# Another order of work inside the attention steps of a fused attention and expert kernel

## The reference

```
Q = LN(x) Wq' + bq;  K = ctx Wk' + bk;  V = ctx Wv' + bv
scores = softmax(Q K' / 4) over 361 keys, per head
x1 = x + tanh(g_x) * (concat_heads(scores V) Wh' + bh)
t  = RMSnorm(LN(x1)) * norm_w;  two best of 8 experts per token
x2 = x1 + tanh(g_f) * sum over 2 experts of w * FFN_expert(t)      (F = 1024, low-rank parts of rank 16)
```

## Time and profile before

| | |
|---|---|
| median of three runs | 527.36 us |
| profiled execution, its own time | 527.83 us |
| its span in the trace | 526.0 us |
| PE busy | 499.5 us, 95% |
| PEld (weight loads) busy | 462.7 us, 88% |
| DVE busy | 348.7 us, 66% |
| POOL busy | 297.2 us, 57% |
| ACT busy | 254.4 us, 48% |
| DMA data moved | 45.83 MB, nearly all of it in the first 270 us |

### The profile page before, as it was taken

The page is one execution under the profiler, slowest core; times in us unless marked ns, Lnnn a source line. Parts: engine busy times, 40 slices in busy tenths (PEclk is TensorE's granted clock), DMA queues, the critical chain, the costliest instruction groups (busy, mean ns, idle before and its releaser), DMA issues.

```text
span 526.0 us, 11848 instructions
## 1 busy us (share of the span) xinstructions
PE 499.5 (95%) x4392; PEld 462.7 (88%) x4392; DVE 348.7 (66%) x774; ACT 254.4 (48%) x578; POOL 297.2 (57%) x350
## 2 busy tenths in 40 slices
PE   8878999999999999999998999999999999999995
PEld 7657888988888888887788899999999999999993
DVE  5857777777788777887547778665376456664443
ACT  4466655555455655557675532444335333333331
POOL 6473565666655655552759956644276434844441
PEclk9999999999999999999899999999999999999998
DMA  7794786877778787755111000010000100001000
GB/s 208 192 260 121 181 203 146 192 179 181 163 170 168 171 193 170 151 135 107 18 17 17 0 1 2 1 32 2 0 2 0 32 1 1 2 0 32 1 0 31
DMA packets 50729, 45.83 MB, mean 87 GB/s; under 512 B 33968, under 2 KB 40148, under 8 KB 50673
## 3 DMA queue, kind: packets, MB, share of 16 engines
q1 hardware_dynamic: 40270, 20.82, 18.0%
q0 software_dynamic: 8128, 21.05, 16.0%
q10 hardware_dynamic: 2274, 3.21, 1.9%
HBM read 20.59 MB, written 6.66 MB: 52 GB/s over the span
## 4 chain that ended last, share of the span: by engine, by line
PE 72%; DVE 8%; ACT 7%; DMA 7%; issue 3%; ACTq 2%; POOL 1%; SPq 0%; POOLq 0%; DVEq 0%
PE bank L1302 12%; PE bank L1194 7%; PE bank L1354 6%; PE bank L1319 6%; PE bank L1306 6%; PE bank L1164 6%; PE bank L1146 6%; DMA QS<-crow 5%; PE bank L1181 4%; PE bank L1334 4%; PE bank L1227 3%; DVE nmax L912 2%; PE bank L1337 2%; ACT pt L510 2%; DMA xs<-x 2%
## 5 line engine op out<-in xcount | busy, mean ns | idle before, releaser
L912 DVE TENSOR_REDUCE nmax<-bank 100x1 f32<-100x361 f32 x256 | 130.6, 524 | 38.0 <-PE bank L1164 32.8
L408 POOL TENSOR_TENSOR awl<-hb,awh 128x400 fp32r<-128x400 f32 x64 | 70.5, 1103 | 102.0 <-ACT awh L609 102.0
L1164 PE MATMUL bank<-KS,QS 96*100 96x362 f32 x256 | 93.4, 367 | 7.4 <-DVE nmax L912 7.2
L510 ACT ACTIVATE pt<-bank 120x400 f32<-120x400 f32 (+1 forms) x192 | 82.8, 506 | 25.7 <-PE bank L1181 25.6
L609 ACT ACTIVATE awh<-hb 128x400 fp32r<-128x400 f32 x64 | 34.5, 539 | 119.5 <-DVE hb L858 119.2
L851 DVE TENSOR_TENSOR hb<-sil,bank 128x400 f32<-128x400 f32 x64 | 36.5, 571 | 83.2 <-PE bank L1319 39.1
L332 POOL DMA_DIRECT2D KS<-kn x64 | 32.0, 508 | 64.9 <-PE bank L1164 53.6
L1164 PEld LDWEIGHTS bank<-KS,QS 96*100 96x100 f32 x256 | 42.2, 166 | 16.9 <-DVE nmax L912 12.2
L1181 PE MATMUL bank<-QS,KS 97*120 97x200 f32 (+1 forms) x384 | 52.6, 273 | 1.6 <-DMA QS<-crow 1.6
L1146 PE MATMUL bank<-wkv,cth 128*120 128x256 f32 (+1 forms) x288 | 50.9, 289 | 0.1
L1181 PEld LDWEIGHTS bank<-QS,KS 97*120 97x120 f32 (+1 forms) x384 | 47.9, 185 | 3.0 <-DMA QS<-crow 3.0
(11 more groups left out here) (193 smaller groups left out, 1123.3 us busy)
## 6 DMA issues: line engine op xcount, KB each, us to landing
KS<-kn SPq DMA_DIRECT2D x128, 90.5 KB, 3.8
KS<-kn POOLq DMA_DIRECT2D x64, 90.5 KB, 3.2
craw<-ctxT POOLq DMA_DIRECT2D x14, 361.0 KB, 6.7
QS<-q_dram POOLq DMA_DIRECT2D x92, 50.0 KB, 5.4
q_dram<-qn ACTq DMA_DIRECT2D x4, 400.0 KB, 4.8
o_dram<-on SPq DMA_DIRECT2D x16, 100.0 KB
xr<-o_dram SPq DMA_DIRECT2D x16, 100.0 KB
y<-xs SPq DMA_DIRECT2D x16, 100.0 KB
```

The costliest lines, as they stand in the source:

```text
L408: nc.gpsimd.tensor_tensor(awl[:, g % 2, slot], hb[:, slot], awh[:, g % 2, slot].bitcast(F32), ALU.subtract).then_inc(m["p_awl"], 1)
L510: nc.scalar.activation(pt[0:TW[t], u, :], pT[u % 3][0:TW[t], 0:CS], ACT.Exp, scale=float(DH) ** -0.5).then_inc(m["act_e"], 1)
L912: nc.vector.tensor_reduce(nmax[:, pos:pos + 1], pS[h % 2][0:S, 0:T], AX.X, ALU.max, negate=True).then_inc(m["dve_s"], 1)
L1164: mm(pS[h % 2][0:S, 0:TP], QS[b % 3][0:96, g, h % 2, j, :], KS[b % 3][0:96, g, j, :], start=True, stop=True).then_inc(m["pe_s"], 1)
```

## The change

It writes a new order into the `body(i)` of ScalarE, VectorE and TensorE for steps 0 to 14, and keeps the old order for step 15 in a `last_step`. On TensorE the transposed units are spread among the heads, one or two at a time; the first head of a step moves ahead of the row turn; K's first half needs only the rounded context (ctx_h) and its second the remainder (ctx_l). On ScalarE the copy `osb` comes first in the step, and the first half's maxima are copied (`row_copy`) and sent (`row_send`) at two places. The rounding of the context of batch i+3 moves from VectorE, where it stood after the 11th reduction, to the end of ScalarE's step (`ctx_high_of`). On VectorE the 16th reduction comes before `first_sum`. An Exp on one column is added to ScalarE's prologue. In step 14 two roundings of weights (`w_high(1)`, `w_high(2)`) stand later. The orders of SP and GpSimd are as they were.

The diff, cut: of the three bodies, the lines that stay and those added are shown; the lines taken out are those of the bodies above. A line with # names the engine.

```diff
...
+            def ctx_high_of(b):
+                act.wait_ge(ctx_sw[b % 2], 16 * (b // 2))
+                act.wait_ge(m["pe_v"], NT * (b - 1))
+                nc.scalar.activation(cth[:, b % 2, 0], craw[:, b % 2], ACT.Copy).then_inc(m["ctx_h"], 1)
...
             def row_out(b, half):
+                row_copy(b, half)
+                row_send(b, half)
+            def row_copy(b, half):
                 act.wait_ge(m["pe_cT"], 2 * b + half + 1)
                 wait(act, ("cr_a", "cr_b")[half], 16 * b)
                 nc.scalar.activation(crow[:, half, :], row_bank(b, half)[0:H // 2, 0:S], ACT.Copy).then_inc(m["act_c"], 1)
+            def row_send(b, half):
                 act.wait_ge(m["act_c"], 2 * b + half + 1)
                 act.dma_start(QS[b % 3][96:97, 2 * half:2 * half + 2, :, :, :].rearrange("o a b c d -> o (a b c d)").bitcast(F32),
                               crow[:, half, :].bitcast(F32)).then_inc(m[("cr_a", "cr_b")[half]], 16)
...
             turned(7)
+            nc.scalar.activation(warm_e[:], nmr[:, 0:1], ACT.Exp).then_inc(m["exp_ok"], 1)
...
# ScalarE, def body(i)
                 if has_o(i):
                     wait(act, "pe_pv", i * UN)
                     wait(act, "pe_oT", i - 1)
                     nc.scalar.activation(osb[:].rearrange("p q s -> p (q s)"), pO[:, 0:CS], ACT.Copy).then_inc(m["act_o"], 1)
+                row_out(i, 1)
+                expo(i, 0)
                 if has_k(i):
                     k_high(b, 0)
+                expo(i, 1)
+                if has_k(i):
                     k_high(b, 1)
+                expo(i, 2)
                 if i == B - 2:
                     w_high(0)
+                expo(i, 3)
+                expo(i, 4)
+                expo(i, 5)
                 if has_k(i):
                     wait(act, "pe_pv", i * UN)
                     v_out(b, 0)
                 if i == B - 2:
                     tokens_high(0, 0)
+                expo(i, 6)
+                row_copy(i + 1, 0)
+                expo(i, 7)
                 if has_k(i):
                     v_out(b, 1)
+                if i == B - 2:
+                    w_high(1)
+                expo(i, 8)
+                expo(i, 9)
+                row_send(i + 1, 0)
                 if i == B - 2:
                     tokens_high(0, 1)
+                expo(i, 10)
+                expo(i, 11)
                 if has_k(i):
                     v_out(b, 2)
+                if has_c(i):
+                    ctx_high_of(i + 3)
...
+            for i in range(0, B - 1):
                 body(i)
+            last_step(B - 1)
...
# VectorE, def body(i)
             def body(i):
                 b = i + 2
+                head(i + 1, 0)
+                head(i + 1, 1)
+                head(i + 1, 2)
+                head(i + 1, 3)
                 if has_k(i):
                     k_low(b, 0)
+                head(i + 1, 4)
+                head(i + 1, 5)
                 if has_k(i):
                     k_low(b, 1)
                 if has_o(i):
                     shares(i)
+                head(i + 1, 6)
+                head(i + 1, 7)
                 if has_o(i):
                     quotient(i)
+                head(i + 1, 8)
                 if i == B - 2:
                     tokens_low(0, 0)
+                head(i + 1, 9)
+                head(i + 1, 10)
+                head(i + 1, 11)
                 if has_y(i):
                     turned_o(i)
+                head(i + 1, 12)
                 if i == B - 2:
                     tokens_low(0, 1)
+                head(i + 1, 13)
+                head(i + 1, 14)
+                head(i + 1, 15)
...
# TensorE, def body(i)
             def body(i):
                 b = i + 2
+                s_head(i + 1, 0)
                 wait(pe, "act_v", min(NT * (i + 2), NT * B))
                 wait(pe, "act_c", 2 * i)
                 row_turn(i, 1)
                 st_unit(i, 0)
+                s_head(i + 1, 1)
                 if has_k(i):
                     if i == 2:
                         pe.wait_ge(m["tbh_ok"], 1)
+                    pe.wait_ge(m["act_c"], 2 * i + 1)
                     wait(pe, "dve_x1", i - 2)
+                    pe.wait_ge(m["ctx_h"], b)
+                    k_part(b, 0, 0, 3)
+                s_head(i + 1, 2)
+                if has_k(i):
                     pe.wait_ge(m["ctx_l"], b + 1)
+                    k_part(b, 0, 3, 6)
+                s_head(i + 1, 3)
                 if has_k(i):
+                    pe.wait_ge(m["act_c"], 2 * i + 2)
                     k_part(b, 1, 0, 3)
+                s_head(i + 1, 4)
+                st_unit(i, 1)
                 if has_k(i):
                     k_part(b, 1, 3, 6)
+                s_head(i + 1, 5)
+                st_unit(i, 2)
+                if has_o(i):
+                    o_turn(i)
+                st_unit(i, 3)
+                st_unit(i, 4)
+                s_head(i + 1, 6)
+                if i == B - 2:
+                    token_turn(0, 0)
+                s_head(i + 1, 7)
+                st_unit(i, 5)
+                if has_k(i):
+                    pe.wait_ge(m["dve_kl"], KT * b + 2)
+                    v_part(b, 0, 0, 3)
+                    v_part(b, 0, 3, 6)
+                st_unit(i, 6)
+                s_head(i + 1, 8)
+                st_unit(i, 7)
+                s_head(i + 1, 9)
+                st_unit(i, 8)
+                if has_o(i):
+                    pe.wait_ge(m["dve_on"], i)
+                else:
+                    pe.wait_ge(m["dve_kl"], KT * b + 1)
+                row_turn(i + 1, 0)
+                if has_k(i):
+                    pe.wait_ge(m["act_v"], NT * b + 1)
+                    v_part(b, 1, 0, 3)
+                s_head(i + 1, 10)
+                if has_k(i):
+                    v_part(b, 1, 3, 6)
+                if has_y(i):
+                    on_turn(i)
+                s_head(i + 1, 11)
+                if i == B - 2:
+                    token_turn(0, 1)
+                st_unit(i, 9)
+                st_unit(i, 10)
+                s_head(i + 1, 12)
+                if has_k(i):
+                    pe.wait_ge(m["act_v"], NT * b + 2)
+                    v_part(b, 2, 0, 3)
+                    v_part(b, 2, 3, 6)
+                s_head(i + 1, 13)
+                st_unit(i, 11)
+                if has_y(i):
+                    y_proj(i)
+                s_head(i + 1, 14)
+                s_head(i + 1, 15)
+                for u in range(UN):
+                    pv_unit(i, u)
+            def last_step(i):
+                pe.wait_ge(m["act_v"], NT * B)
+                pe.wait_ge(m["act_c"], 2 * i)
+                row_turn(i, 1)
+                st_unit(i, 0)
+                st_unit(i, 1)
+                st_unit(i, 2)
+                gate(0)
                 st_unit(i, 3)
                 st_unit(i, 4)
                 st_unit(i, 5)
-                if i == B - 1:
...
+            for i in range(0, B - 1):
                 body(i)
+            last_step(B - 1)
...
```

More of the change, by code:

```diff
@@ L621, in body @@
                 b = i + 2
[L622 to L626, removed]
                 if has_o(i):
@@ L681, in body @@
                 if i == B - 2:
+                    w_high(2)
                     w_high(3)
-                if i == B - 1:
-                    w_high(6)
-            for i in range(0, B + 2):
+            def last_step(i):
+                row_out(i, 1)
+                expo(i, 0)
+                expo(i, 1)
+                expo(i, 2)
+                act.wait_ge(m["pe_pv"], i * UN)
+                act.wait_ge(m["pe_oT"], i - 1)
+                nc.scalar.activation(osb[:].rearrange("p q s -> p (q s)"), pO[:, 0:CS], ACT.Copy).then_inc(m["act_o"], 1)
+                w_high(4)
+                expo(i, 3)
+                expo(i, 4)
+                expo(i, 5)
+                u_high(0, 0)
+                u_high(0, 1)
+                expo(i, 6)
+                expo(i, 7)
+                expo(i, 8)
+                halves_of_weight(0)
+                w_high(5)
+                expo(i, 9)
+                expo(i, 10)
+                expo(i, 11)
+                w_high(6)
+            for i in range(0, B - 1):
                 body(i)
+            last_step(B - 1)
+            act.wait_ge(m["pe_pv"], B * UN)
+            act.wait_ge(m["pe_oT"], B - 1)
+            nc.scalar.activation(osb[:].rearrange("p q s -> p (q s)"), pO[:, 0:CS], ACT.Copy).then_inc(m["act_o"], 1)
             weight_rows(0)
@@ L1027, in body @@
                     variance(i - 3)
-                if has_s(i):
-                    head(i + 1, 15)
                 if i in (11, 12):
@@ L1034, in body, with last_step @@
                     root(0, 6)
-            for i in range(0, B):
+            def last_step(i):
+                logits(0)
+                best_two(0)
+                shares(i)
+                quotient(i)
+                u_low(0, 0)
+                u_low(0, 1)
+                masks(0)
```

(19 more changed lines are left out.)

167 lines of the change are left out of this document (7 added, 160 removed).

## The result

The changed kernel took **525.08 us** in the median of 20 runs (520.45 to 532.05). The kernel before, run beside it, took 529.78 (526.98 to 535.5). The ratio is **0.9893, interval 0.9869 to 0.9917**: faster by 1.1%, some 5.7 us (the medians of all runs are 4.7 apart; the ratio leaves out the slow runs, those of the changed kernel at granted clocks of 0.974 to 0.980).

What follows compares the result with a forecast made beforehand. TensorE's order of work was taken as the bound. Steps 1 to 13 win 0.78 us each (10.1), step 0 2.0, step 14 0.4: 12.5 us off 527.83 gives 515.3 us, with 8 in 10 between 509 and 531.

Steps and rivals of the forecast that it cites:

- TensorE's list and the head waits: TensorE's step: list of 13.2 us stays the floor; the 0.9 us of waits from a late sixth head all go.
- Rival C: Waits only change places, reductions or exponentials holding single units; half of the 0.9 us stays, 521 us; chance 0.12.
- The moved rounding: Context rounding on ScalarE: 0.81 us instead of 0.53, in free time; GpSimd's burst starts 0.1 to 0.2 us into the step.
- Exp in the prologue and step 0: Table load of 1.28 us moves into ScalarE's prologue wait; with the reordering, step 0 wins 2 us.
- a stall of 0.35 us per step: Steps 1 to 13: TensorE's wait for the second half's row of maxima, taking its transfer as 5.15 us.
- The second half's transfer: Transfer of 3.1 KB of maxima before st_unit(i, 6): no stall up to 4.8 us; at the old time, little gain.
- L: Time of the 3.1 KB transfer of the second half's maxima; taken as 5.15 us, bounds under 4.8 and 6.9.
- A: The forecast itself: 515.3 us, own range 510 to 521 with stalls of 0 to 0.8 us; chance 0.55.
- B: The second half's transfer keeps its 5.8 us on average; step 14.17 us, 523.3 us in all; chance 0.18.
- the 0.28 us per step between 14.05 and 14.33: Old order's average excess per step, put down to six waits for the second half's transfer, 3.0 us in all.
- I cost these at nothing: k_stack, query loads and xr on SP's and GpSimd's lists: later or with less slack, still covered, no cost.
- rival D: Transfers issued after the burst's start wait until it drains; steps up to 15.3 us, 538 us, or over 570; chance 0.15.

Runs made afterwards that it cites:

- experiment 4: Changed kernel with the rounding of the context back on VectorE at its old place; ratio to the kernel before 1.018.
- experiment 5: Kernel before with only the rounding of the context moved from VectorE to the end of ScalarE's step; ratio to the kernel before 0.9919.
- experiment 9: Changed kernel without the Exp in ScalarE's prologue, so the table load is back in step 0; ratio to the kernel before 0.9884.
- experiment 13: Changed kernel with the gate's weights loaded in step 12 and the other ten behind step 13's last KS transfers; ratio to the kernel before 0.9826, 522.82 us.
- experiment 1: Changed kernel with transposed units 6 to 11 leaving out the row of maxima and not waiting for its transfer; ratio to the kernel before 0.9842.
- experiment 2: Changed kernel without the row of maxima in units 6 to 11 and with on_turn, turned_o, y_proj later; ratio to the kernel before 0.9796.
- experiment 8: Changed kernel with the second half's row turned after PV's eighth unit and on_turn, turned_o, y_proj later; ratio to the kernel before 0.9871.
- experiment 6: Changed kernel with GpSimd's burst (context, weight, query loads) waiting until the second half's row has landed; ratio to the kernel before 0.9871.
- experiment 7: Changed kernel with the second half's row turned after PV's fourth unit and sent at the end of ScalarE's step; ratio to the kernel before 0.9906.
- experiment 14: Kernel before with the weight loads out of the steps: gate's in step 12, others behind step 13's last KS transfers; ratio to the kernel before 0.9979.
- experiment 12: Changed kernel with all eleven weight loads issued by GpSimd at the end of step 13; ratio to the kernel before 1.0052.
- experiment 10: Changed kernel with eight filler transposes on TensorE before unit 6 of each step; ratio to the kernel before 1.0002.
- experiment 3: Kernel before with units 6 to 11 leaving out the row of maxima and not waiting for its transfer; ratio to the kernel before 0.9986.
- experiment 11: Changed kernel with GpSimd's weight load one place earlier, before ctx_low; ratio to the kernel before 1.0217.

## Why the prediction was right and wrong

**TensorE's list and the head waits: right.** 13.2 us was walked, 13.32 or 13.33 measured in steps 1, 3 and 9. In steps 1 to 13 one head waits for a reduction, 0.42 us in step 12. Rival C, in its form of heads against reductions, is out.

**The moved rounding: right, and worth more than the rest.** GpSimd's weight load starts 0.3 us before the turn that opens the next step, where I had 0.1 to 0.2 behind the first head. Timelines of POOL and ACT after, as the earlier trace rows:

```profile
...
184.47 1.73 POOL L318 TENSOR_TENSOR cth<-craw,cth 128x724 fp32r<-128x724 f32 x1 [4.14 <-ACT cth L468]
186.15 0.57 POOL L344 DMA_DIRECT2D w<-w2T  x1
...
```
```profile
...
37.67 1.28 ACT L574 ACT_TABLE_LOAD   x1
38.97 0.20 ACT L574 ACTIVATE warm_e<-nmr 100x1 f32<-100x1 f32 x1
39.38 0.59 ACT L481 ACTIVATE qn<-bank,bqs 128x400 fp32r<-128x400 f32 x1 [0.20 <-PE bank L1145]
...
```

Experiments 4 and 5 show that this shift of a burst decides the sign: the order alone is slower than before, the rounding alone gives 0.8%.

**Exp in the prologue and step 0: right, a little too large.** The load fits into the old wait, and `qn` comes 0.6 us later than before. Step 0 wins 1.6 us of the 2.0; 0.9 of them are the table load's (experiment 9). The 1.4 us of drain that the prediction held against it show nowhere: 37.67 + 1.28 = 38.95, and the Exp starts at 38.97.

**The failed step: "a stall of 0.35 us per step", in "The second half's transfer" and "The rounding moved to ScalarE".** Measured as the chain of the profile does, from the start of the issue to the last step of the semaphore, L was 5.83 us in the mean of steps 1 to 13 before the change and is 5.45 after it, where I had taken 5.15; the deadline is 5.3 us after the issue, where I had walked 4.8. These two slips nearly cancel. The error is that I priced the stall at the mean. L runs from 4.0 to 7.9 us, and only what lies above the deadline costs: seven of the thirteen transfers are late, and PE waits 6.9 us for six of them, where my term gives 13 x 0.35 = 4.6; two of these waits make up 4.84 of it. Behind those two the clock is at its lower level, which takes 1.6 + 1.7 = 3.3 us more, a term the sum does not have.

The gap of steps 1 to 13, from 13 x 13.55 = 176.2 to 186.75 us, is 10.6: floor 13 x 0.13 = 1.7, waits for the row 2.3, clock 3.3, waits for `xr` and one reduction 0.6. Of the other 2.7, the PEld line has 1.4 more than the PE line, and steps 12 and 13 are longer by some 0.6 for a reason that is no transfer's: they take 14.00 and 13.72 here, and 13.97 and 13.71 in experiment 13. The rest is not resolved. The idle time before the seventh unit is 6.9 / 13 = 0.53 us on average, between the 0.4 that the prediction named as the most for A and the 1 for B.

One reading behind the forecast was loose as well: the 0.28 us per step between 14.05 and 14.33 was put down to the six waits of 3.0 us, which are 0.21 per step. It does not move the sum.

**The second cover that failed: "I cost these at nothing", of `k_stack` and `xr`.** In the change they hardly show (0.2 us), because the wait for the row stands before them. Take it away, and `xr` costs 3.8 us in three waits (experiment 1); take that away too, and it is `KS` (experiments 2, 8). Three transfers share one slack, and the first to be late hides the others. So the mechanism of rival D was there at a smaller price (the row's 7.4 and 7.9 us are longer than any before, 6.9 at most), and it took gain that experiments 1, 6, 7 and 8 were after.

**What is behind it.** The steps' DMA load, and in it the weight loads. With them out of the steps the waits for the row go from 6.9 to 0.3 us, the row takes 4.8 us in the mean and 5.6 at most, and steps 1 to 13 take 10.9 us less than in the kernel before, where 10.1 were predicted, and 8.3 less than the old order with the same move (experiments 13, 14). That rests on one trace each of experiments 12 and 13, which agree. Of the rivals, B (523.3) has the time nearest, and half the reason: the transfer did get shorter, 5.83 to 5.45 in the mean, but by some 0.4 us where I had taken 0.7.

The Trainium skill ("DMA: Bandwidth & Descriptors", section "Queues, rings and completion order") says that each DMA engine takes turns between its queues packet by packet; by that rule a small transfer should wait for about one packet of each other queue. The runs have 1.8 to 2.6 us for the 3.1 KB ahead of the burst (experiment 6) and 4.0 to 7.9 inside it. Which packets it stood behind is not shown, so they neither confirm nor refute the rule.

**What stays open.** Whether the clock falls behind a given wait (below), and so how much of the change's run-to-run spread of 11.6 us comes from it. Why the load of the steps makes one row take 4 us and another 8. What makes steps 12 and 13 longer.

## What to carry to other kernels

Price a wait for a transfer from the spread of its times against its deadline, not from the mean, and add what the clock takes after a long one. When an order is tightened, list all transfers that lived on the air it removes, in the order of their deadlines: removing the first wait uncovers the next. Look for the bulk loads that can leave the tight steps, and for the instruction in front of them on their queue, since moving that one (here a rounding of 0.8 us) moved the whole burst.

## What the runs showed of the hardware

A wait of TensorE for a transfer is followed by the lower clock often, not always. Of the waits of 1.7 us or more that a named transfer ended, eight were followed by it (2.17 and 2.67 in the change; 2.42, 3.21, 2.29, 3.53, 1.74 and 2.37 in experiments 1, 6, 4, 4, 9 and 10). Three were not (1.81 in 4, 2.23 in 9, 2.48 in 8), and none up to 1.5 us was. So the length of the wait alone does not decide it. The 2.48 of experiment 8, with the stretch behind it:

```profile
...
164.90:168.50 3.60, 3.60 (x30) 3.60 (x31) 2.57 (x6) 2.24 (x6) 0.00 (x0) 1.00 0.61 103
...
```

The lower level came without such a wait too. In step 14 or 15 it is found in the profile of before (from 259.5 us, the 1.7 us of the table's last line) and in those of experiments 1, 2, 3, 4, 6, 7 and 8, and no single wait of PE ahead of it in these two steps is longer than 1.1 us. So it is shown that the lower level came behind the two long waits of the change, and only probable that they brought it.

In experiment 11 the clock averaged 0.965 over the span, the lowest of all (0.971 to 0.994 in the other profiles of its order). It has seven waits of 1.9 us or more at the steps' heads, and five of them are followed or accompanied by the lower clock.
